# Ternary feed-forward layers: weights quantised within the layer norm, a new order of tiles, functions of the last part by quarters

## The reference, cut to what matters

```python
def _L0_ffn_ref(x, w_up, w_down):              # layers 1 and 3
    def _ternary_linear(x, w):
        alpha = jnp.mean(jnp.abs(w))
        w_t = jnp.sign(w) * (jnp.abs(w) > 0.5 * alpha).astype(w.dtype)
        w_q = w + jax.lax.stop_gradient(w_t - w)
        rms = jnp.sqrt(jnp.sum(x * x, axis=-1, keepdims=True)) / jnp.sqrt(d)
        return jnp.einsum('bsd,fd->bsf', x / (rms + EPS), w_q)
    h = jax.nn.gelu(_ternary_linear(x, w_up), approximate=False)
    return _ternary_linear(h, w_down)

def _L2_ffn_ref(x, W1, b1, W2, b2):            # layers 9 and 11
    h = jnp.einsum('bsd,fd->bsf', x, _ternary(W1)) + b1
    h = jax.nn.gelu(h, approximate=False)
    return jnp.einsum('bsf,df->bsd', h, _ternary(W2)) + b2
```

## Time and profile before

| | us |
|---|---|
| median of 3 runs | 5742.93 (5742.36 to 5756.35) |
| the profiled execution | 5715.51, its span 5713.8 |
| TensorE busy | 4713.6 (82%) |
| VectorE busy | 3783.7 (66%) |
| ScalarE busy | 3163.8 (55%) |
| layer 1: layer norm, body, to the next layer | 660.1, 696.4, 806.6 |
| layer 3 | 1410.7, 1446.9, 1557.2 |
| layer 9 | 3471.1, 3491.5, 3559.1 |
| layer 11 | 4104.7, 4122.4, 4190.3 |

### The profile page before, as it was taken

One profiled execution on the slowest core, in us unless ns is written; L12 is line 12 of the kernel. 1 busy time (PEld: TensorE's weight loads), 2 busy tenths in 40 slices (PEclk: granted clock), 3 DMA queues, 4 the chain that ended last, 5 costly groups with the idle time before them and its releaser, 6 DMA issues. The chain is left out here.

```text
span 5713.8 us, 91311 instructions
## 1 busy us (share of the span) xinstructions
PE 4713.6 (82%) x33501; PEld 2077.9 (36%) x33596; DVE 3783.7 (66%) x4596; ACT 3163.8 (55%) x6002; POOL 1683.8 (29%) x1468
## 2 busy tenths in 40 slices
PE   5677668998579977799778998589867799799999
PEld 2233223443233336333353333256422344333344
DVE  6899658886589943899448882677539710799400
ACT  5656444766448853488535885444466422488621
POOL 0666315886032215322252220000006400222100
PEclk7899888999789989899898998799989999799999
DMA  0000001111021125211242110000000000111100
GB/s 28 0 1 1 4 28 55 44 45 29 10 72 50 49 74 168 74 49 51 91 150 71 48 52 15 2 10 2 4 10 0 21 0 0 40 38 38 43 0 15
DMA packets 120296, 211.54 MB, mean 37 GB/s; under 512 B 34982, under 2 KB 71442, under 8 KB 118484
## 3 DMA queue, kind: packets, MB, share of 16 engines
q1 hardware_dynamic: 110580, 182.00, 10.4%
q10 hardware_dynamic: 4320, 15.73, 0.9%
q0 software_dynamic: 4992, 8.41, 0.5%
HBM read 153.93 MB, written 52.00 MB: 36 GB/s over the span
## 5 line engine op out<-in xcount | busy, mean ns | idle before, releaser
L958 ACT ACTIVATE l_core_probs<-l_core_ps_scores_b 128x512 f32<-128x512 f32 (+3 forms) x3840 | 1610.1, 508 | 584.6 <-PE l_core_ps_scores_b L866 419.4
L1060 DVE TENSOR_REDUCE l_core_chunk_max<-l_core_ps_scores_a 128x2 f32<-128x1024 f32 (+3 forms) x1280 | 1253.2, 1020 | 84.3 <-PE l_core_ps_scores_a L851 48.9
L866 PE MATMUL l_core_ps_scores_b<-l_q_rows_sb,l_k_rows_sb 64*128 64x512 bf16 (+3 forms) x3840 | 948.7, 333 | 39.9 <-ACT l_core_probs L958 16.6
L851 PE MATMUL l_core_ps_scores_a<-l_k_rows_sb,l_q_rows_sb 64*128 64x512 bf16 (+3 forms) x3840 | 741.2, 345 | 104.0 <-DVE l_core_chunk_max L1060 44.9
L1009 POOL TENSOR_SCALAR_AFFINE_SELECT l_core_probs<-l_core_probs 128x512 f32<-128x512 f32 x512 | 325.8, 636 | 1174.4 <-ACT l_core_probs L958 1169.7
L881 PE MATMUL l_core_ps_acc<-l_core_probs,l_v 128*9 128x512 f32 (+3 forms) x6144 | 648.8, 494 | 15.9 <-ACT l_core_out_sums L932 8.6
L866 PEld LDWEIGHTS l_core_ps_scores_b<-l_q_rows_sb,l_k_rows_sb 64*128 64x128 bf16 x3840 | 304.4, 94 | 702.4 <-ACT l_core_probs L958 614.1
L1060 DVE TENSOR_REDUCE l_core_neg_max<-l_core_ps_scores_a 128x2 f32<-128x256 f32 (+3 forms) x640 | 493.3, 819 | 95.7 <-PE l_core_ps_scores_a L811 93.5
L1931 POOL TENSOR_TENSOR l_scan_bx<-l_xs,l_scan_b_rows 128x1024 f32<-128x1024 f32 x192 | 452.3, 2356 | 224.2 <-DVE l_scan_states L1941 217.9
L1941 DVE TENSOR_TENSOR_SCAN l_scan_states<-l_scan_ps_decay,l_scan_bx 128x1024 f32<-128x1024 f32 x192 | 439.7, 2290 | 40.8 <-POOL l_scan_bx L1931 15.3
L979 POOL TENSOR_TENSOR l_core_probs_decayed<-l_core_probs,l_decay 128x1536 f32<-128x1536 f32 (+2 forms) x160 | 394.0, 2487 | 145.9 <-ACT l_core_probs L958 145.9
(11 more groups left out here) (323 smaller groups left out, 7761.4 us busy)
## 6 DMA issues: line engine op xcount, KB each, us to landing
l_slots_weights<-m_both_dram SPq DMA_DIRECT2D x78, 512.0 KB, 4.6
l_q_rows_sb<-l_q_rows SPq DMA_DIRECT2D x128, 96.0 KB
l_k_rows_sb<-l_k_rows SPq DMA_DIRECT2D x128, 96.0 KB
l_heads_out<-l_core_out_sums SPq DMA_DIRECT2D x300, 32.0 KB
l_q_rows<-l_proj_parts SPq DMA_DIRECT2D x36, 256.0 KB
l_k_rows<-l_proj_parts SPq DMA_DIRECT2D x36, 256.0 KB
l_q_rows_sb<-l_q_rows SPq DMA_DIRECT2D x128, 64.0 KB
l_k_rows_sb<-l_k_rows SPq DMA_DIRECT2D x128, 64.0 KB
```

The lines of the kernel that those rows point to most:

```text
L851: mm = nc.tensor.matmul(slot[:, i, 0:w], qs[n % 3][rows, p, qt * P:(qt + 1) * P], ks[n % 3][rows, p, c * NT:c * NT + w], start=True, stop= ...
L866: mm = nc.tensor.matmul(pb[m % 3][:, 0:w], ks[n % 3][rows, p, kt * P:(kt + 1) * P], qs[n % 3][rows, p, q0:q0 + w], start=True, stop=not diag)
L958: nc.scalar.activation(pt[:, ts % RP, j, 0:w], pb[m % 3][:, 0:w], ACT.Exp, scale=scale).then_inc(b_free, 1)
L1060: nc.vector.tensor_reduce(to, pa[e % 2][:, :, 0:width_a(qt, c)], AX.X, ALU.max, negate=True).then_inc(a_free, 1)
```

## The change

- `layer_norm` gets an argument `ternary` with the weights, their quantised copies and the floor of the scale. With it, VectorE makes the absolute sums before tile 2, thresholds and the quantised up matrix before tile 4, and the quantised down matrix before tile 5. TensorE's weight-sum product stands after its step 4. The variance has three PSUM buffers instead of four, the fourth bank being that product's; so the variance products wait for `ln_ready` and, in the rms form, `cen_free`. All layer norms allocate three more semaphores.
- The body's loops are straight code. TensorE's order becomes up(0), up(1), down(0), mean square(0), up(2), down(1), mean square(1), up(3) and so on. Sums, down products and mean squares have two buffers each with semaphores of their own.
- VectorE normalises tiles 0 and 1 first and tile t+2 after the squares of tile t, and evicts tile t-1 after the squares of tile t. ScalarE's gelu of tile t waits for down(t-2) and the squares of t-2.
- In the tail ScalarE makes the four functions on quarters 0 and 1 together, then all four on quarter 2, then on quarter 3. VectorE multiplies and adds quarter by quarter.

```diff
@@ layer_norm, TensorE
                         pe.wait_ge(sq_ready, t)
-                        nc.tensor.matmul(var[:, (t - 1) % R, :], net.mean[:, :], sq[:, (t - 1) % R, :],
+                        if t > RV:
+                            if rms:
+                                pe.wait_ge(cen_free, t - RV)
+                            pe.wait_ge(ln_ready, t - RV)
+                        nc.tensor.matmul(var[:, (t - 1) % RV, :], net.mean[:, :], sq[:, (t - 1) % R, :],
                                          start=True, stop=True).then_inc(var_ready, 1)
+                    if ternary and t == 4:
+                        pe.wait_ge(abs_ready, 1)
+                        nc.tensor.matmul(pw[:, 0:2], net.ones[:, :], absum[:, :], start=True,
+                                         stop=True).then_inc(wsum_ready, 1)
@@ layer_norm, VectorE
+                def weights(t):
+                    if t == 1:
+                        abs_sums()
+                    elif t == 3:
+                        thresholds()
+                        quantised(0)
+                    elif t == 4:
+                        quantised(1)
+
                 for t in range(TILES):
+                    if ternary and t:
+                        weights(t - 1)
                     dve.wait_ge(rstd_ready, t + 1)
@@ ternary_ffn, TensorE
-                with pe.Fori(0, TILES // 2) as i:
-                    for p in range(2):
...
-                        if p == 1:
-                            down(pe, i, 0)
-                    down(pe, i, 1)
+                for t in range(TILES):
+                    up(t)
+                    if t:
+                        down(t - 1)
                         if rms_in:
+                            mean_square(t - 1)
+                down(TILES - 1)
+                if rms_in:
+                    mean_square(TILES - 1)
@@ ternary_ffn, ScalarE
-                with act.Fori(0, TILES // 2) as i:
-                    for p in range(2):
-                        act.wait_ge(g_free, 2 * i + p + 1)
+                for t in range(TILES):
+                    for half in range(2):
+                        act.wait_ge(up_ready, 2 * t + half + 1)
+                        if t >= 2 and half == 0:
+                            act.wait_ge(dn_ready, t - 1)
+                            if rms_in:
+                                act.wait_ge(sq_chain, 2 * (t - 1))
...
+                    factor((0, 1))
+                    factor((2,))
+                    factor((3,))
@@ ternary_ffn, VectorE
+                    normalised(0)
+                    normalised(1)
+                    for t in range(TILES):
+                        squares(t)
+                        if t + 2 < TILES:
+                            normalised(t + 2)
+                        if t:
+                            evict(t - 1)
+                    evict(TILES - 1)
                     for q in range(4):
+                        scaled(q)
```

More of the change, by code:

```diff
@@ L106, in _, with layer_norm @@
                 sp.wait_ge(stored, 16)
-def layer_norm(net, tag, rms=None, loads=()):
+def layer_norm(net, tag, rms=None, loads=(), ternary=None):
     nc = net.nc
@@ L260, in ternary_ffn @@
[L260 to L272 removed]
+        pm = ps("ms_acc", [P, 2, NT])
@@ L274, in _ @@
+        x_ready, up_ready, gelu_done, sq_chain = (sem(n) for n in ("x_ready", "up_ready", "gelu_done", "sq_chain"))
+        sum_ready, dn_ready, ms_ready, dn_out, ms_out = (sem(n) for n in (
+            "sum_ready", "dn_ready", "ms_ready", "dn_out", "ms_out"))
+        tail_a, tail_b = sem("tail_act"), sem("tail_dve")
+        QT = TILES // 4
+        with nc.Block() as block:
             @block.tensor
             def _(pe):
-                pe.wait_ge(abs_ready, 1)
-                nc.tensor.matmul(pw[:, 0:2], net.ones[:, :], absum[:, :], start=True, stop=True).then_inc(wsum_ready, 1)
@@ new lines, in down, with mean_square @@
+                def down(t):
+                    pe.wait_ge(gelu_done, 2 * t + 2)
+                    if t >= 2:
+                        pe.wait_ge(dn_out, t - 1)
+                    for k in range(FC):
+                        mm = nc.tensor.matmul(py[:, t % 2, :], wt[1][:, k * P:(k + 1) * P], g[:, t % 2, k, :],
+                                              start=(k == 0), stop=(k == FC - 1))
+                    mm.then_inc(dn_ready, 1)
+                def mean_square(t):
+                    pe.wait_ge(sum_ready, t + 1)
+                    if t >= 2:
+                        pe.wait_ge(ms_out, t - 1)
+                    nc.tensor.matmul(pm[:, t % 2, :], net.ones[:, :], ssum[:, t % 2, :], start=True,
+                                     stop=True).then_inc(ms_ready, 1)
@@ new lines, in _ @@
+                if rms_in:
+                    normalised(0)
[4 more added lines that the diff above has]
+                            normalised(t + 2)
+                        if t:
+                            evict(t - 1)
+                    evict(TILES - 1)
+                    for q in range(4):
+                        scaled(q)
+                else:
+                    for t in range(TILES):
+                        tok = slice(t * NT, (t + 1) * NT)
+                        dve.wait_ge(dn_ready, t + 1)
+                        nc.vector.scalar_tensor_tensor(x[:, tok], py[:, t % 2, :], bias[:, 4:5], x[:, tok],
+                                                       ALU.add, ALU.add).then_inc(dn_out, 1)
```

210 lines of the change are left out of this document (91 added, 119 removed).

## The result

| | before | after |
|---|---|---|
| median, us | 5742.65 (5741.69 to 5756.35, 4 runs) | 5673.57 (5668.91 to 5676.03, 4 runs) |
| the profiled execution | 5715.51, span 5713.8 | 5674.63, span 5672.5 |
| TensorE's mean granted clock | 0.923 | 0.927 |

The account below looks back on a forecast made before the run. Hand-overs between engines bound the ternary stages, no engine being full, except TensorE in the bias loop. Gains 5.9x2 + 12.0 + 21.7 + 23.2 = 68.7, less 0.3, take the profiled 5715.5 to 5647.1; plus 27.4, 5674.5 us; range 5661 to 5692.

Parts of the forecast that it names:

- its three parts: Weights 5.9 per rms layer and 12.0 for layers 9 and 11; loop and tail together 21.7 and 23.2 us.
- 0.3 taken off: Whole sum: 0.3 us subtracted for sundry waits of the straight code, 68.7 to 68.4.
- rival 1: Layer norms absorb nothing and grow by 7.4 in all four stages; 19.4 us less gain, 5693.9; chance 0.08.
- The stall of tile 5's products: Rms layer norm: products queued behind the weight sum come up to 3 us later, costed at nothing.
- The barrier term: Rms layer norm's end to up products: barrier 0.80 plus first normalised tile 0.94, 1.74 us.
- Rival 3: Layer norms and up-product starts: TensorE at 1.2 GHz where now 2.4; 5 us over four stages, 5679.5; chance 0.07.
- the 1.53 that the sum took for layer 3: First up products of layer 3: today's slow-clock cost, 8.56-7.03 = 1.53 us, assumed to stay.
- the slack of VectorE: Rms loop: VectorE needs 6.2 us per tile under TensorE's 7.7, so 1.5 us a tile in hand.
- The half-clock start: First up products of the rms body: today's extra 3.04 us in layer 1 stays.
- The chain of a quarter: Tail: ScalarE's four functions on quarter 2 or 3, each waiting for the one before, 4.5 us per quarter.
- The step that I took without a reason: Whole kernel: median stays 27.4 us above the profiled execution, so 5647.1 becomes 5674.5.
- a sign of being wrong as a whole: Stages gain as said, but the untouched rest of the kernel moves by more than 10 us.

Follow-up runs that it names:

- experiment 3: Kernel after, with two or four unused VectorE multiplications added per tile of the rms loop: 5667.56 and 5675.23 us, against 5664.5 without.
- experiment 6: Kernel after plus unused TensorE products where it waits: 5635.24 us; also with rms weights quantised after VectorE's last tile and another tail split: 5627.46 us; after: 5634.72.
- experiment 5: Kernels before and after, both unchanged, profiled on one chip (C): spans 5701.0 and 5632.7 us.

## Why the prediction was right

The mechanism was right in its three parts. The time was 5673.57 against 5674.5; chip C, where both kernels were profiled side by side, lets the steps of layers 1, 9 and 11 be read at the same start of TensorE:

| step, layer 1 | predicted | measured on chip C |
|---|---|---|
| layer norm grows | 2.7 | 33.99 to 36.31: 2.3 |
| from its end to the up products | 10.31 to 1.74 | 10.30 to 1.54 |
| first up product to the stage's end | 99.98 to 78.3 | 99.98 to 77.55 |
| the layer's gain | 5.9 + 21.7 = 27.6 | 28.9 |
| layer 3 | 5.9 + 23.2 = 29.1 | 28.9 |
| layers 9 and 11: layer norm grows | 2.4 | 16.85 to 19.57: 2.7, both |
| layers 9 and 11: the gain | 6.0 and 6.0 | 5.3 and 5.5 |
| sum | 68.4 (0.3 taken off) | 68.7 |

The rows behind layer 1 of this table, before and then after (start and last functions of the layer norm, first up products), and the first up products of layer 9:

```profile
659.75 1.28 ACT L156 ACT_TABLE_LOAD   x1 [28.03 <-PEq L49]
...
692.61 1.13 ACT L192 ACTIVATE l_rms_factor<-l_ln_root 128x512 f32<-128x512 f32 x2
...
704.04 10.02 PE L288 MATMUL l_ps_up<-x_norm,l_q_up 128*128 x16 [7.59 <-DVE x_norm L360]
...
3488.73 8.62 PE L288 MATMUL l_ps_up<-x_norm,l_q_up 128*128 x16 [6.53 <-DVEq L354]
```

```profile
659.66 1.28 ACT L172 ACT_TABLE_LOAD   x1 [28.05 <-PEq L49]
...
694.84 1.13 ACT L208 ACTIVATE l_rms_factor<-l_ln_root 128x512 f32<-128x512 f32 x2
...
697.51 9.82 PE L321 MATMUL l_ps_up<-x_norm,l_q_up 128*128 128x512 f32 x16 [15.98 <-DVE x_norm L390]
...
3428.75 9.52 PE L321 MATMUL l_ps_up<-x_norm,l_q_up 128*128 128x512 f32 x16 [5.13 <-PEq L49]
```

An agreement to 1 us is partly luck. By the interval of the ratio alone the gain lies anywhere from 64 to 78 us, the medians on chip B differ by 77.6, and the four layers of one kernel differ by up to 4.6 together between profiles (466.8, 463.1 and 462.2 before).

**The weights.** ScalarE's lag behind VectorE took up all but 2.3 of the 7.4 us in layer 1 and all but 2.8 in layer 3, as worked out from where VectorE's last mean square would come; rival 1 fell. The stall of tile 5's products was there (2.37 before the weight sum) and cost nothing at the end, as its cover said: once VectorE has begun, it never waits in that layer norm. The barrier term was 0.2 too long: the first up product starts 0.75 behind the first normalised tile (697.51-696.76), not 0.94.

In the bias form the layer norms grew by 2.7, not 2.4, and the gap behind them went from 9.4 to 0.93, where 1.1 was forecast. (In the profiles of the result, layer 9's grew by only 1.7, from 19.37 to 21.07, but there TensorE started slower before than after: 3.75 against 3.06 for the same products.) Two terms were left out of the sum. The up products got dearer by 0.9 and 0.7 on chip C (8.62 to 9.52 and 9.46 to 10.14). And the straight code ends sooner: TensorE stands 1.57 instead of 2.06 before the next layer norm. They partly cancel.

**Rival 3, the clock at the start of the body.** It came true in part. Over three profiles of each kernel, the first up products (x16) of layers 9 and 11 took 8.62 to 9.46 before (9.0 on the mean) and 8.68 to 10.14 after (9.7): 0.7 a stage, under the 1 to 1.5 that the rival had, and within the spread of one kernel. In layers 1 and 3 the mean went the other way (9.8 to 9.4), though TensorE's idle time ahead grew from 7.6 to 16 and more. So the longer idle time of the rms form cost nothing, and the 1.53 that the sum took for layer 3 was one profile's: it was 2.2 on chip C.

**The loop.** 7.72 per tile against 7.73, and no wait; the slack of VectorE was as worked out, by experiment 3. The half-clock start was 9.76-7.03 = 2.7 in layer 1 (3.04 forecast), and experiment 6 shows that it can go.

**The tail.** 12.8 against 13.3. The chain of a quarter took 4.3 (VectorE's starts at 767.68 and 771.98), not 4.5: the estimate of 0.05 per hand-over was too large, and ScalarE ends 10.3 after the last mean square, not 10.8.

**The difference of median and profile.** The step that I took without a reason, that the median stays 27.4 above the profiled execution, was right only in its sum, and that is luck. Of after, profile and median agree within 1.1 us, and its expert layers were long; the profile of before had short ones (353.3 for both layers against 384.6) and its timed runs, by their 5742, most likely long ones: its median is 5742.05 on chip B, 5710.65 and 5714.92 on the others. So most of the 27.4 was most likely a property of the chip and not an overhead of an execution, though on chip C too the profiled execution (5702.7) was 12.2 under the median. Had the two kernels been timed on different chips, the forecast could have missed by some 30 us with every step of it right.

The prediction also named a sign of being wrong as a whole: untouched layers that move by more than 10 us. In the two profiles of the result the expert layers moved by 31.3. On one chip (experiment 5) the twelve untouched layers moved by 0.7 together, so the sign pointed at the comparison and not at the change.

## What to carry to other kernels

Work moved into a stage whose last engine lags is nearly free, up to that lag: work out when the moved engine's last result is due, not how long the moved work is. Give a matmul engine the next tile's products before it asks another engine for the sums of the last one, and check the other engine's queue per tile against it; then split the tail only as far as the engine behind the split can still follow. Before two medians are compared with two profiles, compare the layers that weren't touched; and before a microsecond is given a cause, look how much the same stretch differs between profiles of one kernel.

## What was not expected of the hardware

- The same expert layers last 171 to 179 us on two chips and 184 to 192 on a third, some 30 us of the whole time, with idle time of TensorE that the trace puts down to nothing (16.2 us in layer 5 of the profile of after).
- Behind the same 2.15 us of idle and the same code, the same centred products (x4) of one kernel took 1.95, 3.06 and 3.75 us in three executions. Behind the same 5.1 of idle, the first up products (x16) of its layer 9 took 8.68, 9.52 and 10.11.
- ScalarE's table for the gelu, loaded in every turn of the loop before and once per stage in straight code, had a price in neither: 1.28 us under TensorE's products.
